# Attention with a gated feed-forward layer: rope steps spread over more units, and gate and up products placed between the last units' values

## The reference, cut to what matters

```python
xn = _layernorm(x)                      # x: (1, 2048, 256), all float32
# attention: 16 heads; nope 128, rope 64, value 128, lora 64
q = (xn @ wq).reshape(b, s, H, QH).transpose(0, 2, 1, 3)
q_nope, q_pe = (q[..., :NOPE], q[..., NOPE:])
kva = xn @ wkv_a
ckv, k_pe = (kva[..., :LORA], kva[..., LORA:])
ckv = ckv * rsqrt(mean(ckv * ckv) + EPS) * kv_norm_scale
kv = (ckv @ wkv_b).reshape(b, s, H, NOPE + VD).transpose(0, 2, 1, 3)
k_nope, v = (kv[..., :NOPE], kv[..., NOPE:])
q_pe, k_pe = _rope(q_pe, cos, sin), _rope(k_pe[:, None], cos, sin)
scores = einsum('bhqd,bhkd->bhqk', [q_nope, q_pe], [k_nope, k_pe]) * scale
attn = softmax(where(causal, scores, min))
s = einsum('bhqk,bhkd->bhqd', attn, v).transpose(0, 2, 1, 3).reshape(b, s, H * VD) @ wo
# feed-forward on the same xn, 704 inner columns
g = silu(((silu((xn @ gate_w.T) * gate_s) * ((xn @ up_w.T) * up_s)) @ down_w.T) * down_s)
out = x + s * g
```

## Time and profile before

| | |
|---|---|
| median of the runs | 1112.69 us |
| the profiled execution: its own time | 1112.44 us |
| its span from the first to the last instruction | 1110.6 us |
| TensorE busy | 976.1 us (88%), mean granted clock 0.943 |
| ScalarE busy | 787.7 us (71%) |
| VectorE busy | 728.5 us (66%) |
| GpSimd busy | 711.0 us (64%) |
| setup, until the first scores | 75.5 us |
| seven pairs, from the first scores to those of unit 112 | 797.5 us |
| last pair and the values behind it, until the first gate product | 127.5 us |
| feed-forward and output | 110.1 us |

### The profile page before, as it was taken

The page is one execution under the profiler, slowest core; times in us unless marked ns, Lnnn a source line. Parts: engine busy times, 40 slices in busy tenths (PEclk is TensorE's granted clock), DMA queues, the critical chain, the costliest instruction groups (busy, mean ns, idle before and its releaser), DMA issues.

```text
span 1110.6 us, 26363 instructions
## 1 busy us (share of the span) xinstructions
PE 976.1 (88%) x10560; PEld 842.8 (76%) x10560; DVE 728.5 (66%) x1093; ACT 787.7 (71%) x1157; POOL 711.0 (64%) x514
## 2 busy tenths in 40 slices
PE   5738898989898989898989899998898898779998
PEld 5726786878787878786878787877787777768887
DVE  6546666767776767576767676777676776663134
ACT  1427878788887887787778878878888787763232
POOL 3455958486948694877487857776786667722331
PEclk8759998999999999999999989999899999889999
DMA  5018998989999999999989999999999989992001
GB/s 166 9 48 150 170 178 166 172 163 191 170 177 174 179 173 172 173 178 169 180 165 171 183 166 179 180 173 173 176 167 177 179 159 199 190 180 76 1 19 58
DMA packets 591978, 170.23 MB, mean 153 GB/s; under 512 B 574064, under 2 KB 585968, under 8 KB 591856
## 3 DMA queue, kind: packets, MB, share of 16 engines
q1 hardware_dynamic: 587376, 167.89, 83.7%
q10 hardware_dynamic: 4480, 0.66, 0.4%
HBM read 15.41 MB, written 2.10 MB: 16 GB/s over the span
## 4 chain that ended last, share of the span: by engine, by line
PE 27%; SPq 22%; POOL 16%; ACT 10%; issue 8%; DMA 8%; DVE 7%; ACTq 1%; POOLq 0%
SPq L465 10%; PE s_ps L620 10%; PE s_ps L522 9%; SPq L457 6%; DMA q_swap<-q_pe 5%; POOL hl L1102 5%; ACT hl L725 5%; SPq L451 4%; POOL pe L1102 4%; POOL q_swap L1102 4%; PE slot_ps L522 3%; ACT prob L802 2%; ACT QB_hi L725 2%; DVE part_max L941 2%; DVE hl L950 2%
## 5 line engine op out<-in xcount | busy, mean ns | idle before, releaser
L1102 POOL TENSOR_TENSOR hl<-prob,hl 128x1024 f16<-128x1024 f32 (+4 forms) x256 | 402.1, 1571 | 184.1 <-ACT hl L725 173.1
L802 ACT ACTIVATE prob<-s_ps,neg_max 128x1024 f32<-128x1024 f32 (+7 forms) x384 | 318.0, 862 | 95.1 <-DVE neg_max L944 74.4
L941 DVE TENSOR_REDUCE part_max<-s_ps 128x1 f32<-128x1024 f32 (+7 forms) x256 | 245.5, 988 | 176.6 <-PE s_ps L620 159.4
L725 ACT ACTIVATE hl<-prob 128x1024 f16<-128x1024 f32 (+7 forms) x384 | 296.3, 806 | 9.9 <-DMA pT<-hl 7.9
L636 PE MATMUL o_ps<-v,pT 128*128 128x65 f16 x2176 | 232.0, 195 | 7.1 <-DMA pT<-hl 5.7
L637 PE MATMUL o_ps<-v,pT 128*128 128x64 f16 x2176 | 232.5, 197 | 0.0
L638 PE MATMUL o_ps<-v,pT 128*128 128x65 f16 x2176 | 231.3, 193 | 0.0
L636 PEld LDWEIGHTS o_ps<-v,pT 128*128 128x128 f16 x2176 | 206.5, 98 | 7.8 <-DMA pT<-hl 6.3
L950 DVE TENSOR_TENSOR hl<-prob,hl 128x1024 f16<-128x1024 f32 (+3 forms) x128 | 158.3, 1236 | 78.0 <-ACT hl L725 76.5
L638 PEld LDWEIGHTS o_ps<-v,pT 128*128 128x128 f16 x2176 | 205.7, 100 | 0.0
L637 PEld LDWEIGHTS o_ps<-v,pT 128*128 128x128 f16 x2176 | 205.1, 98 | 0.0
(11 more groups left out here) (182 smaller groups left out, 1974.8 us busy)
## 6 DMA issues: line engine op xcount, KB each, us to landing
q_swap<-q_pe SPq DMA_DIRECT2D x128, 64.0 KB, 2.1
pT<-hl SPq DMA_TRANSPOSE x256, 4.9
wq_sb<-in_L_attn_wq_dram SPq DMA_DIRECT2D x8, 384.0 KB, 4.1
acc<-in_L_attn_x_dram SPq DMA_DIRECT2D x4, 512.0 KB, 6.3
wo_sb<-in_L_attn_wo_dram SPq DMA_DIRECT2D x8, 256.0 KB, 4.0
x_in<-in_L_attn_x_dram SPq DMA_DIRECT2D x1, 2048.0 KB, 8.3
out_dram<-y SPq DMA_DIRECT2D x8, 256.0 KB, 2.1
wkvs<-in_L_attn_wkv_b_dram SPq DMA_DIRECT2D x8, 128.0 KB, 4.3
```

What stands on the lines that cost most here:

```text
L725: return nc.scalar.activation(dst, src, ACT.Copy)
L802: nc.scalar.activation(prob_of(u, m), score_bank(u, m), ACT.Exp, bias=neg_max[:, r:r + 1]).then_inc(exp_done, 1)
L941: nc.vector.tensor_reduce(part_max[:, u % 2, m:m + 1], src, AX.X, ALU.max).then_inc(part_done, 1)
L1102: return lambda: nc.gpsimd.tensor_tensor(dst, a, b, op)
```

## The change

Jobs and rope steps get other positions. The second query job of group 2 goes from position 1 to 0, the first from 0 to 15 of the pair before, and those of the other groups one position earlier too, so SyncE's four swap DMAs stand one unit earlier as well. Rope step 0 moves one unit ahead of steps 1 and 2. wpe_lo joins wpe_hi at position 6. wkvT moves from 5 to 4 and wabs from 6 to 5, wqT from 3 to 4; outP3a and outP3b go from 4 to 3, outP2b from 15 to 0 of the next pair. In the last pair one feed-forward weight job pair moves from 11 to 12. `gate_up` takes one product instead of a group, and products 0 and 1 stand behind TensorE's round 127, 2 and 3 behind round 128, ahead of the values of units 126 and 127. VectorE's part of products 0 and 1 stands ahead of its last normalisation. The last output jobs are attached to other products.

```diff
-JOBS_BEFORE = {2: ["outT3"], 4: ["outP3a", "outP3b"]}
-JOBS_OWN = {0: ["qA2"], 1: ["qB2"], 2: ["qA1"], 3: ["qB1"], 5: ["wvo"], ...
-JOBS_NEXT = {3: ["wqT"], 5: ["wkvT"], 6: ["wabs"], 8: ["qA3"], 9: ["qB3"], 10: ["qA0"], 11: ["qB0"]}
+JOBS_BEFORE = {0: ["outP2b"], 2: ["outT3"], 3: ["outP3a", "outP3b"]}
+JOBS_OWN = {0: ["qB2"], 1: ["qA1"], 2: ["qB1"], 5: ["wvo"], ...
+JOBS_NEXT = {4: ["wqT", "wkvT"], 5: ["wabs"], 7: ["qA3"], 8: ["qB3"], 9: ["qA0"], 10: ["qB0"], 15: ["qA2"]}
+EARLY = {PU * PAIRS - 1: (0, 2), PU * PAIRS: (2, 4)}
+OUT_LAST = {0: ("outP2a", PAIRS - 1), 1: ("outP2b", PAIRS - 1), 5: ("outT3", PAIRS - 1), 7: ("outP3a", PAIRS - 1), 8: ("outP3b", PAIRS - 1)}
...
-POOL_NEXT = {1: ["wkvs"], 6: ["wpe_hi"], 7: ["wpe_lo"], 10: rope(3), 11: ["A3lo", "B3lo"], 12: rope(0), 13: ["A0lo", "B0lo"]}
-POOL_OWN = {2: rope(2), 3: ["A2lo", "B2lo"], 4: rope(1), 5: ["A1lo", "B1lo"]}
+POOL_NEXT = {1: ["wkvs"], 6: ["wpe_hi", "wpe_lo"], 9: rope(3)[:1], 10: rope(3)[1:], 11: ["A3lo", "B3lo"] + rope(0)[:1], 12: rope(0)[1:],
+             13: ["A0lo", "B0lo"]}
+POOL_OWN = {1: rope(2)[:1], 2: rope(2)[1:], 3: ["A2lo", "B2lo"] + rope(1)[:1], 4: rope(1)[1:], 5: ["A1lo", "B1lo"]}
...
+            def gate_up(j):
+                n, it = divmod(j, IT)
+                if j >= 2:
+                    pe_eng.wait_ge(hid_done, j - 1)
+                if j == 0:
+                    pe_eng.wait_ge(exp_done, 3 * NU)
+                    pe_eng.wait_ge(dve_freed, after("dve", FFN_DOWN[-1]))
...
+                if j in OUT_LAST:
+                    out_job(*OUT_LAST[j])
...
                 for name in jobs_at(u):
                     job(name)
...
+                for j in range(*EARLY.get(u, (0, 0))):
+                    gate_up(j)
...
+            for j in range(max(stop for _, stop in EARLY.values()), NG * IT):
+                gate_up(j)
+                if j >= 2 * IT - 1 and j % IT == IT - 1:
+                    down(j // IT - 1)
...
             for u in range(-1, NU + LAG + 1):
+                if u == NU + LAG:
+                    for j in range(2):
+                        hidden(j)
                 if u >= LAG + 1 and head_of(u - LAG - 1) == 1:
                     normalise(u - LAG - 1)
```

More of the change, by code:

```diff
@@ L140, in jobs_at @@
         last = pair == PAIRS - 1
-        if pair > 0:
-            jobs += [(name, pair - 1) for name in JOBS_BEFORE.get(k, ())]
-        jobs += [(name, pair) for name in JOBS_OWN.get(k, ()) if (name, pair) not in OUT_LAST]
+        jobs += [(name, pair - 1) for name in JOBS_BEFORE.get(k, ())] if pair > 0 else [(name, pair) for name in JOBS_FIRST.get(k, ())]
+        jobs += [(name, pair) for name in JOBS_OWN.get(k, ()) if (name, pair) not in OUT_LAST.values()]
         if last:
@@ L160 @@
 MAIN_END = dict(MAIN.count)
-for name in OUT_LAST:
+for name in OUT_LAST.values():
     MAIN.add(name, KIND[name[0]])
@@ L659, in setup_job @@
                 last.then_inc(slot_ready, 1)
+            def gate_up(j):
[5 more added lines that the diff above has]
+                    pe_eng.wait_ge(dve_freed, after("dve", FFN_DOWN[-1]))
+                c = slice(n * BANK, (n + 1) * BANK)
+                i = slice(it * P, (it + 1) * P)
+                for w in range(2):
+                    last = exact(s_ps[:, 2 * (j % 2) + w, :], [
+                        (upT_hi[:, w, k, i], upT_lo[:, w, k, i], xT_hi[:, k, c], xT_lo[:, k, c]) for k in range(KE)])
+                last.then_inc(gu_ready, 1)
+                if j in OUT_LAST:
+                    out_job(*OUT_LAST[j])
             pe_eng.wait_ge(pool_done, POOL.after("ident"))
@@ L864, in _ @@
                 nc.scalar.activation(silu_g[:, j % 2, :], s_ps[:, 2 * (j % 2), :], ACT.Silu).then_inc(silu_done, 1)
-                if j < len(OUT_LAST):
+                if j in OUT_LAST:
                     out_job(*OUT_LAST[j])
@@ L1052, in _, with hidden @@
             keys_lo(3)
+            def hidden(j):
+                dve.wait_ge(silu_done, j + 1)
+                if j >= 2:
+                    dve.wait_ge(hid_lo_done, j - 1)
+                nc.vector.tensor_tensor(hid[:, j % 2, :], s_ps[:, 2 * (j % 2) + 1, :], silu_g[:, j % 2, :], ALU.mult).then_inc(hid_done, 1)
+                if j in OUT_LAST:
+                    out_job(*OUT_LAST[j])
             for u in range(-1, NU + LAG + 1):
+                if u == NU + LAG:
+                    for j in range(2):
+                        hidden(j)
                 if u >= LAG + 1 and head_of(u - LAG - 1) == 1:
@@ L1078, in _ @@
             for j in range(NG * IT):
-                dve.wait_ge(silu_done, j + 1)
                 if j >= 2:
[L1081 to L1084, removed]
+                    hidden(j)
                 if j % IT == 4 and j >= 2 * IT:
@@ L1232, in _ @@
                 n, it = divmod(j, IT)
+                if j == 0:
+                    pool.wait_ge(pool_done, POOL.after(("rest", NU - 1)))
                 pool.wait_ge(hid_hi_done, j + 1)
```

8 lines of the change are left out of this document (4 added, 4 removed).

## The result

| | before | after |
|---|---|---|
| median of the runs | 1111.44 us (4 runs) | 1094.49 us (4 runs) |
| ratio, 95% interval | | 0.985, 0.982 to 0.987 |
| the profiled execution: its span | 1110.6 us | 1091.5 us |
| seven pairs | 797.5 us | 783.2 us |
| from unit 112's first scores to the end | 237.6 us | 236.9 us |

The kernel is faster by 17 us, where 40.8 were forecast; direction and range were right, the size was not. Of the 19 us between the two profiled executions, 4.1 lie in the setup, which the change does not touch. In the other profiles of this study the first scores start anywhere between 67.8 and 76.0 us, so that part is chance. The pairs gained 14.3 us, 2.0 each, where 5.4 each were forecast.

The account below looks back on a forecast made before the run. It took TensorE, stalled behind ScalarE and GpSimd's rope, as the bound, with SyncE's queue next. Pairs 37.8, last pair 1 and products 2 made 40.8 us off 1112.4: about 1072 us, range 1045 to 1099.

Parts of the forecast that it names:

- What bounds the kernel: In the pairs, TensorE idles about 10.8 of 113.9 us, behind ScalarE's exponentials, which wait for GpSimd's rope.
- The rope: GpSimd's rope: step 0 and the swap wait leave the chain; nearly all of ScalarE's 69.5 us of waits go.
- its own sign: Sign that the rope forecast is right: ScalarE's wait for the rope falls from 69.5 to under 20 us.
- The jobs: Moved query, weight and output jobs in the pairs: priced at 0, between -0.5 and +0.5 us a pair.
- What a pair costs then: Pair falls from 113.9 to 108.5 us, between TensorE alone, about 105, and SyncE's queue, 109.7; seven pairs give 37.8 us.
- the queue's sum: SyncE's queue, full through a pair: 16 units at 6.1 us, four swaps at 2.54, loads 1.9, together 109.7 us.
- The last pair: Last pair, with two rope groups and a feed-forward load through the same queue: gains 1 us.
- The four products: Early gate and up products at the end of the kernel: gain 2 us, between -0.5 and +4.5.
- The rivals: Four other outcomes: queue keeps up, 1042 us (0.22); late load, 1088 (0.16); no change, 1112 (0.05); dearer transposes, 1148 (0.07).
- (b): Rival, chance 0.16: queue at full price, late wkvs load keeps the position 3 rope stall; pair 110.5 us, total 1088.
- (d): Rival, chance 0.07: transposes cost more without pauses; at 6.7 us a unit a pair is 119.3 us, total 1148.

Follow-up runs that it names:

- experiment 2: Changed kernel with only the query jobs, rope, outP0b and outP2b moved; outP1, outP3 and weights' jobs as before the change, no early products: 1098.67 us.
- Experiments 3: Changed kernel with only the high halves transposed, which stand in for the low halves in the product: 1090.85 us.
- 4: Two versions of the changed kernel, 16 of 512 columns kept: in GpSimd's second and third rope products, 1064.79 us; in ScalarE's three split copies, 1066.07 us.
- experiment 8: Changed kernel with query jobs, swaps and rope steps one more unit earlier from the second pair on, GpSimd's weight steps from 6 to 5: 1075.36 us.

## Why the prediction was wrong, step by step

**What bounds the kernel** was right in kind: TensorE idle 10.8 us of a pair, behind ScalarE, behind the rope.

**The rope** was right by its own sign (16.3 us left, under 20 forecast), and by the place that I worked out: at position 3 nothing or little is left of 3.5 us. I worked out that place alone. That both step 0 and the wait for the swap leave the chain holds for the groups split at 3 and 11. For those at 5 and 13, step 0 stands at 3 and 11; I said that it delays the next low half by 1.3 us, "which the two units until the values hide", and overlooked that the rope's own last steps stand behind that low half. There 1.2 to 1.6 us remained.

**The jobs** at 0 were right within what the runs tell, for the jobs that the change moved: experiment 2.

**What a pair costs then** is the step that failed. It put the pair at 108.5, between TensorE alone at about 105, with "some 3.5 us of stalls that stay" and some 2 us back from the slow clock, and SyncE's queue at 109.7. The stalls that stayed were 9.1 us, hardly anything came back from the clock (busy 102.8 us after 103.1), and the queue had pauses. Each of the two bounds, though, turned out near the truth once the chain was out of the way: 104.6 us a pair with half of the transposes (TensorE, forecast 105), 108.5 to 109.3 with all of them (forecast 108.5), and 1074 to 1075 us against the 1072 forecast; that is another schedule, so it does not make the forecast right for this one. What I had left out was a third limit: the chain of low halves, rope, split and exponential across GpSimd, VectorE and ScalarE. It holds TensorE up around positions 4 to 6 and 12 to 14, and it kept the pair at 112 us. I had put it at nothing once the waits shrank. Experiments 3, 4 and 8 show it: half of the transposes gains nothing in the pairs, 1.3 to 2.5 us of the chain's work taken out at four places of a pair gains 28 to 30 us, and removing the two waits that were left in a pair gains 19 us, 2.7 a pair.

That a wait of ScalarE's of 1.2 us reaches TensorE is read in the timeline at 722 to 734: behind it come three copies, two high halves and the next exponential, and TensorE has no job to do meanwhile.

Why the queue's sum was no bound for this kernel: the price of 6.1 us a unit is that of a queue that is behind. The time of an issue is no fixed cost: for one shape, the first transpose of a unit, it has a median of 1.94 us in the changed kernel, with extremes of 1.3 and 4.4:

```profile
L460 SPq DMA_TRANSPOSE pT<-hl x128: 1316/1942/4396, 82.6 to 972.4; - x128
```

With half of the blocks in each and half of the bytes in flight the median was 1.23, and 16 of 128 were longer than 1.5. Sixteen units at the full price assumed what was to be shown, that the queue is never waiting for its inputs. The cited rule of the Trainium skill (Perfetto Trace Analysis, What "DMA-bound" means) asks for solid DMA slices; in the changed kernel they were not solid through a whole pair (9.6 us of pauses).

**The last pair** at +1: the stretch from unit 112's to unit 127's first scores went from 106.6 to 107.5 us, so -1, within what two pairs differ by.

**The four products** at +2: 1.3 to 1.4. From the end of the weight job on VectorE to product 4 it was 17.8 us by my sum and is 19.1. The parts:

```profile
973.55 1.28 DVE L891 TENSOR_TENSOR downT_lo<-slot_ps,downT_hi 128x512 fp32r<-128x512 f32 x2
```

```profile
974.98 0.47 PE L525 MATMUL s_ps<-xT_hi,upT_hi 128*128 128x512 f32 x1 [2.75 <-DVE downT_lo L891]
...
993.95 0.50 PE L525 MATMUL s_ps<-xT_hi,upT_hi 128*128 128x512 f32 x1 [1.33 <-DVE hid L1061]
```

The wait for `hid` at product 4 is there with 1.33 us (forecast 1.3). What is over comes from product 0: at a granted clock of 0.61 it takes 4.4 us to the next instruction in place of 2.8, and the rest of the sum was some 0.3 too long.

**The rivals.** None was what happened. (b) is nearest in time (1088) and named waits left at the rope, but at position 3 and by a late load; neither is there. (d), dearer transposes, would have shown as a kernel slower than before, and no run was slower than before.

## What to carry to other kernels

When a wait shrinks, ask at each of its places what stands in front of the producer's last step, and move the whole chain until the result is early, not merely less late: here one unit earlier gave 17 us, with the early products, and two units 36 to 37. A step moved ahead has left the chain only if its engine pauses somewhere between it and the result. Before a resource is called the next bound, check that its price was not measured while it was already behind, and look for a chain through several engines that is nearly as long; none of its engines is near full (ScalarE 92 of 112 us). Halving a transfer's work and leaving its results out tells in one run whether it bounds the schedule at hand; the same test told no for the pairs of one schedule and yes, 34 us, in the next. Sums over all pairs hide where the time goes: TensorE is never idle at positions 8 to 11, where only less work for it could gain anything.

## What was not expected of the hardware

VectorE's low half of 128x896 takes 1.08 to 1.09 us in 20 of its 32 instances in the changed kernel, and 1.13 to 2.46 us in twelve. All twelve begin while a low half or rope step of GpSimd is running, and all end 0.94 to 0.96 us after that instruction ends: the one at 724.01 ends at 726.47, GpSimd's first low half beside it at 725.51:

```profile
723.37 2.14 POOL L1113 TENSOR_TENSOR hl<-prob,hl 128x1024 f16<-128x1024 f32 x1
```

It is the same in the kernel before (7 instances) and in that of experiment 8 (15). So this instruction of VectorE waits for the GpSimd instruction that was there first. One that begins after it, even if it runs beside it for nearly all of its time, leaves it at 1.09. That adds 1.4 us to the chain at 724. No run moved VectorE's low half away from GpSimd's, so its share of the 112 us is open.

An idle stretch filled with matmuls kept the clock at 1.00 where it was 0.63 to 0.78 in five pairs of seven, and the time did not change; at position 7 a lower clock cost 2.9 us in full. Whether a half clock seen in the rows is a cost is told by what stands behind it: idle time that can take it up (position 0), or work without a gap (positions 8 to 11).
